# Two transposed inputs loaded already exchanged instead of turned on TensorE, with a new written order and a new set-up order

## The reference, cut to what matters

```python
x = _layernorm(x + _L0_gnn_ref(x, adj, Wq, Wk, Wv, Wo, bo))     # masked attention, 4 heads of 64
x = _layernorm(x + _L1_gnn_ref(x, adj, W, bW, attn, A_w, ...))  # gated layer, 4 heads
x = _layernorm(x + _L2_gnn_ref(x, adj, map_w, q_w, k_w, ...))   # masked softmax times a cosine cut, 8 heads of 32
x = _layernorm(x + _L3_gnn_ref(x, adj, Wq, Wk, Wv, Wo, bo))     # masked attention again

# attention: q, k, v = x @ Wq, x @ Wk, x @ Wv
sim = where(adj, q k^T * scale, -max);  out = softmax(sim) v @ Wo + bo
# gated layer, for each head h
Wh = x W[h]^T + bW[h];  A_mat = tanh(where(adj, (Wh attn[h]) Wh^T, 0))
hp = relu(A_mat Wh);  ha = concat(hp) @ A_w^T;  hf = x @ fc_w^T
coeff = sigmoid(hf g1_w^T + ha g2_w^T + gbias);  out = hf coeff + ha (1 - coeff)
```

## Time and profile before

| what | value |
|---|---|
| median of 3 executions | 2617.25 us (2616.52 to 2620.95) |
| the profiled execution: its time | 2622.45 us |
| the profiled execution: span, first to last instruction | 2620.5 us |
| mean granted TensorE clock | 0.991 |
| PE busy | 2558.4 us, 98% |
| DVE busy | 2007.6 us, 77% |
| ACT busy | 1409.9 us, 54% |
| POOL busy | 918.1 us, 35% |
| one turn of the loop | 78.3 us |

### The profile page before, as it was taken

The page is one execution under the profiler, slowest core; times in us unless marked ns, Lnnn a source line. Parts: engine busy times, 40 slices in busy tenths (PEclk is TensorE's granted clock), DMA queues, the critical chain, the costliest instruction groups (busy, mean ns, idle before and its releaser), DMA issues.

```text
span 2620.5 us, 63291 instructions
## 1 busy us (share of the span) xinstructions
PE 2558.4 (98%) x22097; PEld 2291.7 (87%) x22097; DVE 2007.6 (77%) x6629; ACT 1409.9 (54%) x3925; POOL 918.1 (35%) x988
## 2 busy tenths in 40 slices
PE   7999999999999999999999999999999999999996
PEld 7888888898888898888898888898888898888884
DVE  4477878877878877878877877877877777877875
ACT  2355555655555655555655555655655655654653
POOL 3233333343333343333343333343333343333331
PEclk8999999999999999999999999999999999999998
DMA  4000000000000000000000000000000000000000
GB/s 136 7 1 12 11 11 1 10 10 10 10 10 0 10 10 10 10 10 0 10 10 10 10 10 0 10 10 10 10 10 0 10 10 10 10 10 1 11 7 9
DMA packets 44490, 29.90 MB, mean 11 GB/s; under 512 B 21264, under 2 KB 44048, under 8 KB 44432
## 3 DMA queue, kind: packets, MB, share of 16 engines
q1 hardware_dynamic: 44432, 29.13, 3.8%
HBM read 20.73 MB, written 8.39 MB: 11 GB/s over the span
## 4 chain that ended last, share of the span: by engine, by line
PE 84%; ACT 4%; DVE 3%; issue 1%; POOL 0%; ACTq 0%; DVEq 0%; POOLq 0%
PE bank L474 21%; PE bank L476 19%; PE bank L475 19%; ACT arena L606 4%; PE bank L1451 4%; PE bank L531 3%; PE bank L540 3%; PE bank L463 3%; PE bank L1441 3%; PE bank L551 3%; PE bank L1431 2%; PE bank L1462 2%; DVE arena L690 1%; PE bank L1261 1%; DVE arena L647 0%
## 5 line engine op out<-in xcount | busy, mean ns | idle before, releaser
L405 POOL TENSOR_SCALAR l_ve<-l_mv 128x2 f32<-128x2 f32 x128 | 29.0, 226 | 1031.2 <-DVE l_mv L390 1030.9
L474 PE MATMUL bank<-arena_r 128*128 128x256 f32 x1024 | 303.3, 296 | 0.2
L1605 ACT ACTIVATE b<-b,s_sh 128x256 f32<-128x256 f32 x496 | 246.7, 502 | 88.4 <-DVE s_sh L647 88.3
L476 PE MATMUL bank<-arena_r 128*128 128x256 f32 x1024 | 289.0, 282 | 0.0
L475 PE MATMUL bank<-arena_r 128*128 128x256 f32 x1024 | 289.0, 282 | 0.0
L1885 POOL TENSOR_TENSOR arena_r<-a,arena_r 128x512 fp32r<-128x512 f32 x128 | 166.2, 1299 | 329.6 <-ACT arena_r L1541 329.5
L1880 POOL TENSOR_TENSOR arena_r<-a,arena_r 128x512 fp32r<-128x512 f32 x128 | 166.2, 1299 | 171.6 <-ACT arena_r L1547 171.5
L474 PEld LDWEIGHTS bank<-arena_r 128*128 128x128 f32 x1024 | 194.6, 190 | 22.8 <-issue 22.2
L1775 DVE SCALAR_TENSOR_TENSOR b<-bank,b 128x256 f32<-128x256 f32 x496 | 184.8, 421 | 30.9 <-ACT b L1605 25.7
L475 PEld LDWEIGHTS bank<-arena_r 128*128 128x128 f32 x1024 | 195.2, 191 | 0.0
L476 PEld LDWEIGHTS bank<-arena_r 128*128 128x128 f32 x1024 | 194.8, 190 | 0.0
(11 more groups left out here) (304 smaller groups left out, 9060.5 us busy)
## 6 DMA issues: line engine op xcount, KB each, us to landing
x_in<-in_x SPq DMA_DIRECT2D x32, 256.0 KB, 2.8
out<-x SPq DMA_DIRECT2D x32, 256.0 KB, 2.1
adj_a<-in_adj SPq DMA_DIRECT2D x32, 64.0 KB, 2.5
adj_b<-in_adj SPq DMA_DIRECT2D x32, 64.0 KB, 1.9
a<-in_L_gnn_W SPq DMA_DIRECT2D x4, 256.0 KB, 3.4
b<-in_L_gnn_A_w SPq DMA_DIRECT2D x1, 1024.0 KB, 7.8
arena<-in_L_gnn_attn SPq DMA_DIRECT2D x4, 256.0 KB, 7.1
...
```

The source lines that it names most:

```text
L474: pe.matmul(out, w[0], x[0], start=first, stop=False)
L476: return pe.matmul(out, w[1], x[0], start=False, stop=last)
L1605: last = act.activation(R.e[h // QUAD][:, n, it, :], R.e[h // QUAD][:, n, it, :], ACT.Exp, bias=S.sh[:, it, h:h + 1], scale=-1.0, accum_ou ...
```

## The change

The host hands over two more arrays, `x_t` and `adj_t`, in which rows and columns of every graph are exchanged. SP loads them in plain form for each graph (256 KB and 64 KB) beside `x` and `adj`. `a_x_t` is no stage of PE any more: ACT and DVE make the halves straight from the loaded tile in SBUF. `g_adj_t` is no stage of PE and DVE any more: POOL casts the loaded tile to `g_adj_t` directly. In set-up the products with `attn` come first and `A_w` is loaded and turned later; POOL no longer begins `FILL` with `b_keep`. All lists are written anew, and the loop's body begins at another stage.

ACT's list around `g_p_2`, POOL's around `b_rstd` and `g_a_3`, DVE's around the attention masks:

```diff
 ACT
-("b_exps_4", 3), ("b_exps_5", 3), ("g_p_1", 2), ("g_s_3", 2), ("b_exps_6", 3), ("g_a_3", 2), ("g_wh_3", 2), ("b_exps_7", 3), ("g_p_2", 2), ("b_copy_6", 3), ("b_copy_4", 3), ("g_p_3", 2),
+("b_exps_4", 3), ("g_p_1", 2), ("b_exps_5", 3), ("g_s_3", 2), ("g_wh_3", 2), ("b_exps_6", 3), ("g_a_3", 2), ("b_exps_7", 3), ("b_copy_4", 3), ("g_p_2", 2), ("b_copy_6", 3), ("g_p_3", 2),
 POOL
-("g_a_3", 2), ("g_wh_3", 2), ("b_sums", 3), ("b_rstd", 3), ("b_mask", 2), ("g_x_ha", 2), ("d_bias", 3), ("a_bias", 1), ("g_rstd", 2), ("g_adj", 1), ("a_rstd", 1), ("b_inorm", 2),
+("g_wh_3", 0), ("b_sums", 1), ("g_a_3", 0), ("b_rstd", 2), ("g_x_ha", 1), ("a_bias", 0), ("d_bias", 2), ("a_mask", 0), ("g_rstd", 1), ("a_rstd", 0), ("g_adj", 0), ("b_inorm", 1), ("b_mask", 1),
 DVE
-("g_gate", 2), ("a_x_t", 1), ("g_mix", 2), ("g_sum", 2), ("g_stats", 2), ("d_v", 3), ("d_mask_0", 3), ("d_mask_1", 3), ("d_mask_2", 3), ("d_mask_3", 3), ("d_norm_p_0", 3), ("a_v", 1), ("g_norm_out", 2), ("d_norm_p_1", 3), ("d_probs_1", 3), ("a_mask_0", 1),
+("g_gate", 2), ("g_mix", 2), ("g_sum", 2), ("g_stats", 2), ("d_v", 3), ("a_x_t", 1), ("d_mask_0", 3), ("d_mask_1", 3), ("d_mask_2", 3), ("g_norm_out", 2), ("d_mask_3", 3), ("d_norm_p_0", 3), ("d_norm_p_1", 3), ("d_probs_1", 3), ("a_v", 1), ("a_mask_0", 1),
```

The stages, set-up and the loads:

```diff
+                if stage == "a_x_t":                                   # ACT
+                    act.wait_ge(x_t_loaded.sem, x_t_loaded.all(g))
+                    if later(g):
+                        act.wait_ge(G.p_psum.sem, G.p_psum.all(g - 1))
+                    act.activation(A.xt[0], x_t_in[:, :, :], ACT.Copy).then_inc(A.x_t_hi.sem, 1)
+                if stage == "a_x_t":                                   # DVE
+                    dve.wait_ge(A.x_t_hi.sem, A.x_t_hi.at(g))
+                    dve.tensor_tensor(A.xt[1], x_t_in[:, :, :], A.xt[0].bitcast(F32), ALU.subtract).then_inc(A.x_t_sb.sem, 1)
                 elif stage == "g_adj":                                 # POOL
-                    pool.wait_ge(adj_a_loaded.sem, adj_a_loaded.all(g))
+                    pool.wait_ge(adj_t_loaded.sem, adj_t_loaded.all(g))
                     if later(g):
-                        pool.wait_ge(G.adj_psum.sem, G.adj_psum.all(g - 1))
+                        pool.wait_ge(G.a_f.sem, G.a_f.all(g - 1))
                     apart(pool)
-                    pool.tensor_copy(G.adj_bf[:, :, :], adj_a[:, :, :]).then_inc(G.adj_bf_ready.sem, 1)
+                    pool.tensor_copy(G.adj_t[:, :, :], adj_t_in[:, :, :]).then_inc(G.adj_sb.sem, 1)
...
             for h in range(HG):                                        # pe_setup
                 step(lambda b: pe_transpose_rows(pe, b, W.w[:, h, :, :], C.ident))
-            for cc in range(HG):
-                step(lambda b: pe_transpose_rows(pe, b, W.a_w[:, :, cc * DIM:(cc + 1) * DIM], C.ident))
             pe.wait_ge(wa_loaded, 16 * len(loads_a))
             for h in range(HG):
                 r_done = step(lambda b: mm_pairs(b, W.attn[:, h, :, :], lambda kc: W.w[:, h, kc, :]))
             for h in range(HG):
                 step(lambda b: mm_pairs(b, W.w[:, h, :, :], lambda kc: W.r[:, h, kc, :]), needs=r_done)
+            pe.wait_ge(wh_loaded, 16 * len(loads_h))
+            for cc in range(HG):
+                step(lambda b: pe_transpose_rows(pe, b, W.a_w[:, :, cc * DIM:(cc + 1) * DIM], C.ident))
+            pe.wait_ge(wf_loaded, 16 * len(loads_f))
...
             with sp.Fori(2, GRAPHS - 1) as t:                          # SP; load_a now begins with x_t
                 store(t - 2)
                 load_a(t + 1)
                 load_b(t)
+                load_t(t + 1)
...
 FILL, PE
-        ("a_x_t", 0), ("w_map", 0), ("a_k", 0), ("a_q", 0), ("a_v", 0), ("a_scores_0", 0), ("a_scores_1", 0),
+        ("w_map", 0), ("a_q", 0), ("a_k", 0), ("a_v", 0), ("a_scores_0", 0), ("a_scores_1", 0), ("w_qk", 0),
```

More of the change, by code:

```diff
@@ L52 @@
     "PE": [
[L53 to L57, removed]
@@ L66 @@
     ],
     "ACT": [
[4 rows of a table removed]
-        ("b_copy_4", 3), ("g_p_3", 2), ("b_relu_1", 3), ("g_ha", 2), ("g_ha_t", 2), ("d_x_t", 3), ("a_x_t", 1),
[3 rows of a table removed]
-        ("g_x_t", 1), ("g_c", 1), ("b_q", 2), ("g_z_0", 1), ("b_k", 2), ("b_unit_t", 2), ("g_z_1", 1), ("g_wh_0", 1),
+        ("b_exps_4", 3), ("g_p_1", 2), ("b_exps_5", 3), ("g_s_3", 2), ("g_wh_3", 2), ("b_exps_6", 3), ("g_a_3", 2),
+        ("b_exps_7", 3), ("b_copy_4", 3), ("g_p_2", 2), ("b_copy_6", 3), ("g_p_3", 2), ("b_relu_1", 3), ("g_ha", 2),
+        ("g_ha_t", 2), ("d_x_t", 3), ("a_x_t", 1), ("g_gate", 2), ("d_q", 3), ("d_k", 3), ("d_exps_0", 3),
@@ L144 @@
+        ("g_gate_x", 2), ("g_gate", 2), ("d_k", 1), ("d_q", 1), ("d_v", 1), ("d_scores_0", 1), ("d_scores_1", 1),
[3 rows of a table added]
+        ("a_out", 3), ("b_m", 2), ("b_sem", 2), ("b_k", 2), ("g_x_t", 3), ("b_q", 2), ("g_c", 3), ("g_wh_0", 3),
+        ("g_z_0", 3), ("g_c_t", 3), ("g_wh_1", 3), ("b_unit_t", 2), ("g_z_1", 3), ("b_scores_0", 2),
     ],
@@ L160 @@
-        ("d_exps_1", 0), ("a_q", 2), ("a_k", 2), ("a_exps_0", 2), ("a_exps_1", 2), ("d_probs_0", 0), ("d_exps_2", 0),
-        ("d_exps_3", 0), ("a_exps_2", 2), ("a_exps_3", 2), ("a_probs_0", 2), ("a_probs_2", 2), ("d_probs_2", 0),
-        ("a_o_copy", 2), ("d_o_copy", 0), ("b_x_t", 1), ("g_x_t", 2), ("b_q", 1), ("b_k", 1), ("g_c", 2),
-        ("g_z_0", 2), ("b_unit_t", 1), ("g_wh_0", 2), ("g_z_1", 2),
[4 rows of a table added]
+        ("g_p_2", 0), ("a_x_t", 1), ("g_p_3", 0), ("g_ha", 0), ("g_ha_t", 0), ("g_gate", 0), ("a_q", 1), ("a_k", 1),
@@ new lines @@
+        ("b_x_t", 0), ("a_exps_0", 1), ("a_exps_1", 1), ("a_exps_2", 1), ("a_probs_0", 1), ("a_exps_3", 1),
+        ("a_probs_2", 1), ("a_o_copy", 1), ("b_k", 0), ("b_unit_t", 0), ("b_q", 0), ("g_x_t", 1), ("g_z_0", 1),
[5 rows of a table added]
+        ("d_x_t", 0), ("a_x_t", 2), ("g_ha", 1), ("d_q", 0), ("d_k", 0), ("g_ha_t", 1), ("d_exps_0", 0),
+        ("g_gate", 1), ("d_exps_1", 0), ("a_q", 2), ("a_k", 2), ("a_exps_0", 2), ("a_exps_1", 2), ("d_exps_2", 0),
+        ("d_probs_0", 0), ("d_exps_3", 0), ("a_exps_2", 2), ("a_exps_3", 2), ("d_probs_2", 0), ("a_probs_0", 2),
@@ new lines @@
+        ("a_mask_0", 1), ("a_mask_1", 1), ("b_x_t", 0), ("a_mask_2", 1), ("a_norm_p_0", 1), ("a_mask_3", 1),
+        ("a_probs_1", 1), ("a_norm_p_1", 1), ("b_m", 0), ("a_probs_3", 1), ("b_square", 0), ("a_o_copy", 1),
+        ("a_sum", 1), ("a_stats", 1), ("b_unit", 0), ("a_norm_out", 1), ("b_sem", 0), ("g_x_t", 1), ("b_mask_0", 0),
[5 rows of a table added]
+        ("g_a_3", 1), ("g_p_1", 1), ("g_p_2", 1), ("b_scale", 0), ("b_sum", 0), ("b_stats", 0), ("b_norm_out", 0),
+        ("g_p_3", 1), ("d_x_t", 0), ("g_ha_t", 1), ("a_x_t", 2), ("g_diff", 1), ("d_mask_0", 0), ("g_gate", 1),
[3 rows of a table added]
@@ L204 @@
     "PE": [
-        ("g_ha_1_1", 1), ("b_values_1", 2), ("g_ha_2_1", 1), ("b_out", 2), ("g_ha_2_0", 1), ("g_ha_3_1", 1),
-        ("g_ha_3_0", 1), ("g_hf", 1), ("g_ha_t", 1), ("g_gate_x", 1), ("d_x_t", 2), ("g_gate", 1), ("a_x_t", 0),
-        ("d_q", 2), ("d_k", 2), ("d_v", 2), ("d_scores_0", 2), ("d_scores_1", 2), ("a_q", 0), ("a_k", 0),
[3 rows of a table removed]
-        ("b_m", 1), ("b_q", 1), ("b_sem", 1), ("g_x_t", 0), ("g_adj_t", 0), ("b_k", 1), ("g_c", 0), ("g_z_0", 0),
[6 rows of a table removed]
-        ("b_out", 1), ("g_ha_2_1", 0), ("g_ha_3_1", 0), ("g_ha_3_0", 0), ("g_ha_t", 0), ("g_gate_x", 0), ("d_x_t", 1),
@@ L246 @@
-        ("b_q", 1), ("g_x_t", 0), ("g_c", 0), ("g_z_0", 0), ("b_k", 1), ("b_unit_t", 1), ("g_z_1", 0), ("g_wh_0", 0),
[4 rows of a table removed]
-        ("b_copy_6", 1), ("g_p_3", 0), ("b_relu_1", 1), ("g_ha", 0), ("g_ha_t", 0), ("d_x_t", 1), ("g_gate", 0),
-        ("d_k", 1), ("d_q", 1), ("b_x_t", 0), ("d_exps_0", 1), ("d_exps_1", 1), ("d_exps_2", 1), ("d_exps_3", 1),
-        ("b_k", 0), ("d_probs_0", 1), ("d_probs_2", 1), ("d_o_copy", 1), ("b_q", 0), ("b_unit_t", 0), ("b_exps_0", 0),
+        ("b_exps_4", 3), ("b_exps_5", 3), ("g_p_1", 2), ("g_wh_3", 2), ("g_s_3", 2), ("b_exps_6", 3), ("g_a_3", 2),
@@ new lines @@
+        ("b_exps_7", 3), ("g_p_2", 2), ("b_copy_6", 3), ("b_copy_4", 3), ("g_p_3", 2), ("a_x_t", 1), ("b_relu_1", 3),
+        ("g_ha", 2), ("g_ha_t", 2), ("d_x_t", 3), ("g_gate", 2), ("d_k", 3), ("d_q", 3), ("d_exps_0", 3),
+        ("d_exps_1", 3), ("d_exps_2", 3), ("d_exps_3", 3), ("a_k", 1), ("a_q", 1), ("d_probs_0", 3), ("d_probs_2", 3),
+        ("a_exps_0", 1), ("a_exps_1", 1), ("a_exps_2", 1), ("a_exps_3", 1), ("a_probs_0", 1), ("b_x_t", 2),
+        ("d_o_copy", 3), ("a_probs_2", 1), ("a_o_copy", 1), ("g_x_t", 1), ("g_c", 1), ("b_k", 2), ("g_z_0", 1),
[5 rows of a table added]
```

263 lines of the change are left out of this document (129 added, 134 removed), and 245 rows, old and new, of tables (DRAIN, FILL, ORDER).

## The result

The changed kernel takes 2639.83 us in the median of 4 runs (2638.61 to 2642.12). The kernel before took 2619.1 beside it; the ratio is 1.0079, 95% interval 1.0067 to 1.0091. So the change made it slower, by 21 us or 0.8%, where the prediction had 2614 and a range up to 2630. The case that came nearest is the fifth, which had a chance of 0.08 and a time of 2633; the measured time lies 7 us above that too. In the profiled execution the span is 2636.6 us and the clock 0.993.

The account below looks back on a forecast made before the run. PE was taken as the bound, busy 78.00 of 78.36 us a turn. Terms summed to +0.04 us a graph, about +1 over 31 graphs, with -5 for set-up: about 2619 profiled, 2614 median; range 2596 to 2630.

Parts of the forecast that it names:

- The fifth case: POOL's `g_x_ha` makes the second normalization wait for a port: +0.68 us a graph, 2633 in total; chance 0.08.
- the upper end: Bound of +0.48 us a graph for PE's wait at `d_x_t` behind the normalizations; the lower was +0.03.
- the moved `d_x_t`: PE from `g_ha_t` to `g_gate`: `d_x_t` waits 0.68 us for `b_norm_out`; term taken as +0.40 a graph.
- a_x_t: Its four transposes leave PE's list, with the slower first product behind them: -0.43 us a graph.
- g_adj_t and g_c: Gated layer's start on PE: `g_adj_t`'s transposes go, -0.28 us a graph; `g_c` then waits, +0.20.
- Switches: PE changing between transposes and plain products: `g_c_t` and `b_unit_t` now stand apart, +0.10 us a graph.
- g_p_3: PE's wait for the copies of `g_p_2`, which shares its bank: nothing to 0.3 us, taken as +0.05.
- Set-up: Before the loop: `attn` products first, `A_w` later, `a_x_t(0)` off PE; net -5 us, bounds -3 and -6.
- the first attention product: Sign in the changed profile: the first product of the first attention starts near 43 instead of 47.88.
- the sixth case: Set-up order brings nothing, because `attn` lands late and DVE's copies pace it: 2618; chance 0.04.

Follow-up runs that it names:

- `b_mask` back: Changed kernel with POOL running `b_mask` between `b_rstd` and `g_x_ha` again, in the loop only; median 2628.5 us.
- POOL waiting: Changed kernel with POOL's `g_x_ha` waiting until `b_norm_out` has ended, all lists in the changed order; median 2617.1 us.
- the base: Changed kernel with POOL's `g_x_ha` waiting until `b_norm_out` has ended and ACT taking `g_p_2` before `b_copy_4`; medians 2610.3 and 2610.0 us.
- the old lists: Changed kernel's loads and set-up with the lists of the kernel before, removed stages taken out, POOL's `g_adj` moved in `FILL`; median 2617.3 us.
- both halves: Changed kernel with POOL's `g_x_ha` split into two instructions of 256 columns each instead of one of 512; median 2636.8 us.
- the last kernel: The base, but POOL's `g_x_ha` waits only for the first of the two normalizations of `b_norm_out`; median 2605.4 us.

## Why the prediction was wrong

The step that failed is "I stay near the upper end and take +0.40" for the moved `d_x_t`. Two rows gave the length of the pair, one with nothing on POOL beside it and one with `b_mask`, which cost 0.39. I kept 0 and 0.39 as the bounds of the price, although the instruction that now stood there was another one. It cost 0.95. The wait before `d_x_t` was 1.24 and not 0.68, and the term +1.08 (`b_out` to `d_q` 9.59 against 8.15, less 0.71 for the `g_ha` that moved in, plus 0.35 for `a_x_t`, which has its own term). The fifth case had priced just this at +1.04; its chance was too low. It had the hold itself right and the order wrong: in it `g_x_ha` begins 0.03 behind the first normalization and holds the second, while in the trace it began 0.05 ahead and held the first. Its total of 2633 stayed 7 us short, as it counted 5 us for set-up and 0.05 for `g_p_3`, which the next points take up. (I also counted 31 turns; the loop makes 27.) The runs with `b_mask` back (-0.52) and with POOL waiting (-0.92) give the two differences that follow from the pair alone, 0.55 and 0.94.

By the other terms, from one turn of each kernel (78.29 and 79.20):

- **a_x_t**: -0.43 said, -0.42 measured. It came through only because `d_x_t` moved ahead of `g_gate_x` with it. With `d_x_t` behind `g_gate_x` 0.25 went into the wait of `d_q`. I had not priced that cover.
- **g_adj_t and g_c**: -0.28 + 0.20 = -0.08 said, -0.05 measured (from `g_x_t` through `g_z_0` 5.37 against 5.42); `b_sem` takes 1.72 to the next start.
- **Switches**: +0.10 said, -0.01 measured (3.67 against 3.68 for `g_wh_1`, `g_c_t`, `b_unit_t` and `g_z_1`).
- **g_p_3**: +0.05 said, +0.27 measured; the upper bound was 0.3. ACT's order explains it: with `g_p_2` ahead of `b_copy_4` again the 0.27 were gone and the turn fell by 0.25. I had the parts (0.85 against 0.61 and 0.2) and rounded them toward nothing.
- **Rest**: -0.18 for the other `g_ha`, +0.10 for `g_p_2`, +0.07 for `b_q` (it waits for `g_x_t`'s turn behind the normalization that the cast holds), some small ones: together near 0.

The sum is +0.91 in these turns and 0.86 in the mean, where +0.04 was said. **Set-up**: the first attention product starts at 41.28, where 43 was said. But in the 13 profiles of the changed kernel and of those made from it, it lies between 39.2 and 45.5, and the first `d_x_t` that I count turns from between 415 and 426, against 423.7 in the one profile of before. All that lies outside the 27 turns (the median's difference less 27 times the turn's) adds up to -2.5 us in the changed kernel, -1.0 and +0.2 in the two runs of the base, and -0.6 with the old lists. So the -5 was not there. The order of set-up brings nothing that the runs can show, and the sixth case (chance 0.04) was right in that part and half right in the reason: `attn` did not land late (its products start at 10.54), but DVE's copies do pace the stretch. That there is a gain of some 2 us from PE's earlier start is possible and was not measured alone.

The Trainium skill, "SBUF — State Buffer", section "Who interferes with whom", says that DVE and GpSimd share one pair of ports under an exclusive lock. It names two kinds of DVE instruction that contend for it, one in a two-port mode and one with two inputs in SBUF; whoever issues first has the pair for the whole instruction and the other blocks fully. The profile doesn't show in which mode the normalizations ran. The trace agrees wherever POOL began first: `g_x_ha` (1.36 beside 1.27, begun 0.05 ahead), the cast (0.69 beside 0.60, begun 0.07 ahead) and both halves, with each hold ending 0.15 behind POOL's instruction. Where DVE began first, it lost nothing beside `g_x_ha` in the last kernel and beside L738 in the changed one. That the other then blocks shows only in part: L738 took 0.84 instead of 0.74, but `g_x_ha` its usual 1.29 although 0.15 of it lay beside the normalization. The trace doesn't agree for `b_mask`: DVE began first by 0.05 and still lost 0.40, and the second normalization, which began 0.68 behind the start of `b_mask` and ended before it, lost nothing.
